# Picking fourteen embedding tables in teams of two, with shared compares, instead of fifteen one by one

## The reference, cut to what matters

```python
e = jnp.stack([tbl_0[ids[:, 0]], ..., tbl_31[ids[:, 31]]], axis=1)   # 512 x 32 x 128
dot = jnp.einsum('bnd,bmd->bnm', e, e)
flat = dot[:, iu, ju]                                               # pairs i < j
h = jnp.concatenate([flat, dense_ctx], axis=1)
h = jnp.maximum(h @ W_top1 + b_top1, 0.0)                            # 512 x 512
h = jnp.maximum(h @ W_top2 + b_top2, 0.0)                            # 512 x 256
y = h @ W_top3
```

## Time and profile before

| | |
|---|---|
| median of three runs without a profile | 124.33 us (123.89 to 124.69) |
| the profiled execution, first to last instruction | 148.7 us |
| busy in the profiled execution: PE, DVE, ACT, POOL | 121.4, 75.2, 78.8, 71.3 us |
| PE's mean granted clock, as a share of 2.4 GHz | 0.919 |

### The profile page before, as it was taken

The page is one execution under the profiler, slowest core; times in us unless marked ns, Lnnn a source line. Parts: engine busy times, 40 slices in busy tenths (PEclk is TensorE's granted clock), DMA queues, the critical chain, the costliest instruction groups (busy, mean ns, idle before and its releaser), DMA issues.

```text
span 148.7 us, 2677 instructions
## 1 busy us (share of the span) xinstructions
PE 121.4 (82%) x1028; PEld 99.5 (67%) x1028; DVE 75.2 (51%) x196; ACT 78.8 (53%) x79; POOL 71.3 (48%) x76
## 2 busy tenths in 40 slices
PE   5889979989999689499995464321999899999993
PEld 3457758868788468378884452111999798999971
DVE  2999999989897399496800000000333033223301
ACT  3588899999997897799950510000143302210022
POOL 3877749787787477378775577772000000000000
PEclk9999999999999999959999776555599999999999
DMA  5998736666667356793221011211056441024000
GB/s 144 275 338 267 234 100 204 204 216 225 217 219 235 110 178 195 232 324 113 55 53 52 23 53 53 53 53 35 4 146 202 136 126 35 4 78 127 10 0 1
DMA packets 11150, 19.81 MB, mean 133 GB/s; under 512 B 2353, under 2 KB 7473, under 8 KB 11138
## 3 DMA queue, kind: packets, MB, share of 16 engines
q1 hardware_dynamic: 7522, 13.74, 29.8%
q0 software_dynamic: 2176, 4.46, 10.3%
q10 hardware_dynamic: 1440, 1.44, 3.0%
HBM read 17.54 MB, written 2.13 MB: 132 GB/s over the span
## 4 chain that ended last, share of the span: by engine, by line
PE 64%; ACT 15%; issue 11%; another core or an unknown queue 5%; DVE 2%; DMA 2%; ACTq 0%
PE two_ps L564 15%; PE two_ps L566 14%; PE two_ps L606 8%; PE two_ps L625 8%; ACT onehot L442 8%; PE free_ps L606 7%; ACT emb L421 5%; PE free_ps L636 3%; PE turn_ps L574 3%; PE two_ps L636 2%; ACT high L421 2%; DMA id_sb<-row_ids 2%; PE two_ps L641 1%; PE turn_ps L625 1%
## 5 line engine op out<-in xcount | busy, mean ns | idle before, releaser
L307 POOL DMA_INDIRECT rows<-tables,row_no x64 | 66.6, 1040 | 26.5 <-issue 14.9
L564 PE MATMUL two_ps<-onehot,high 128*128 128x512 f32 x128 | 52.7, 412 | 7.4 <-ACT onehot L442 4.3
L566 PE MATMUL two_ps<-onehot,low 128*128 128x512 f32 x128 | 50.9, 397 | 0.0
L442 ACT ACTIVATE onehot<-narrow 128x2560 fp32r<-128x2560 f16 (+3 forms) x16 | 35.5, 2226 | 4.8 <-PE two_ps L566 3.0
L564 PEld LDWEIGHTS two_ps<-onehot,high 128*128 128x128 f32 x128 | 24.8, 193 | 16.7 <-issue 10.4
L566 PEld LDWEIGHTS two_ps<-onehot,low 128*128 128x128 f32 x128 | 24.8, 194 | 4.7
L326 DVE TENSOR_SCALAR onehot<-pick_id,own_row 128x512 fp32r<-128x512 int16 x53 | 23.0, 479 | 4.4 <-PE two_ps L566 3.5
L316 DVE TENSOR_TENSOR low<-home,high 128x512 fp32r<-128x512 f32 (+1 forms) x36 | 22.4, 625 | 3.8 <-issue 3.7
L336 DVE TENSOR_SCALAR narrow<-pick_id,own_row 128x512 f16<-128x512 int16 x75 | 22.4, 365 | 0.0
L606 PE MATMUL two_ps<-emb 128*64 128x64 f32 x240 | 12.9, 247 | 9.4 <-issue 9.3
L196 DVE COPY home<-free_ps 128x512 f32<-128x512 f32 x4 | 2.8, 692 | 33.8 <-remote 29.8
(11 more groups left out here) (37 smaller groups left out, 54.5 us busy)
## 6 DMA issues: line engine op xcount, KB each, us to landing
home<-picked SPq DMA_DIRECT2D x10, 512.0 KB, 3.6
home<-picked SPq DMA_DIRECT2D x4, 640.0 KB
pick_id<-pick_ids SPq DMA_DIRECT2D x13, 128.0 KB, 3.7
w_sb<-w SPq DMA_DIRECT2D x3, 512.0 KB
dot_out<-home SPq DMA_DIRECT2D x10, 128.0 KB, 2.4
rows<-tables,row_no POOLq DMA_INDIRECT x64
dot_out<-home ACTq DMA_DIRECT2D x6, 128.0 KB, 2.6
pairs<-dot_out SPq DMA_DIRECT2D x10, 64.0 KB, 2.0
```

The costliest lines, as they stand in the source:

```text
L307: pool.indirect_dma_start(rows[:, k % ROWS_HELD, i, :], None, lone if one_table else tables, bass.IndirectOffsetOnAxis(ap=id_sb[:, 0, c:c ...
L442: act.activation(onehot[:, at:at + n, :], narrow[:, t % 2, n0:n0 + n, :], ACT.Copy).then_inc(onehot_act, n)
L564: pe.matmul(out, high[:, at, D * k:D * (k + 1)], onehot[:, c % HOT, :], start=(k == 0), stop=False)
L566: pe.matmul(out, low[:, at, D * k:D * (k + 1)], onehot[:, c % HOT, :], start=False, stop=(k == KR[t] - 1)).then_inc(picked_done, 1)
```

## The change

Fourteen tables are picked (118 chunks, three of the tables with 10), and 18 are gathered. `MORE` becomes 2, so the first tile of a block has two gathers, a block has 18 and all have 72. Tile 13 now ends with gather 49, tile 14 with gather 53, the last one with 71.

The fourteen tables form eight teams: one table, six pairs, one table. A team's tables of equal chunk count go step by step together. One DVE compare of 1024 ids makes the one-hot matrices of both tables for a step, in either way; one id load serves a team. 68 steps are left. `BY_ACT` is 0 for the first team, 4 for one and 3 for the others: 22 steps. Two teams are held (`HELD`), three id sets, 8 one-hot steps and a ring of 7 narrow ones. `pace` counts steps. PE turns one tile in the middle and one at the end of a team. The last table's result is copied out in two parts, 128 samples by ACT and the rest by DVE. To save room, the narrow tile shares its place with `h1`, `h2` and the output row, and `w2` with the ids, so SP loads `w2` once DVE has made all its compares.

```diff
-PICK = 15
+PICK = 14
+TEAMS = [[0]] + [[t, t + 1] for t in range(1, PICK - 1, 2)] + [[PICK - 1]]
+KT = [KR[team[0]] for team in TEAMS]
...
-BY_ACT = [2, 4, 5, 5, 5, 5, 5, 5, 5, 5, 5, 6, 6, 6, 6]
+BY_ACT = [0, 3, 3, 3, 3, 3, 4, 3]
...
-TURNED = PICK - 1
-LAG = 2
-TABLES_HELD, IDS_HELD, HOT, ROWS_HELD = 3, 4, 16, 7
+TURNED = 2 * NT - 2
+HELD, IDS_HELD, HOT, NARROW, ROWS_HELD = 2, 3, 8, 7, 7
...
 def pace(c):
-    return min(51 * c // 20 - 10, CHUNK0[PICK])
+    blocks = min(51 * c // 20 - 10, CHUNK0[PICK])
+    return blocks if blocks < KT[0] else (blocks + KT[0]) // 2
...
+            for g in range(2, NT):
+                if g >= IDS_HELD:
+                    sp.wait_ge(onehot_dve, DVE0[g - IDS_HELD + 1])
...
+                ids_load(sp, g)
+                for i in range(len(TEAMS[g])):
+                    table_load(g, i)
...
+            sp.wait_ge(onehot_dve, DVE0[NT])
+            sp.wait_ge(narrow_ready, ACT0[NT])
             sp.dma_start(w2_sb[:, :, :], w2.rearrange("(c p) n -> p c n", p=P)).then_inc(weights_in, 16)
...
-                    dve.tensor_scalar(onehot[:, c % HOT, :], pick_id[:, t % IDS_HELD, :], own_row[:, i, k:k + 1], None,
+                    dve.tensor_scalar(onehot[:, c % HOT, 0:n, :], pick_ids_of[:, g % IDS_HELD, 0:n, :],
+                                      own_row[:, STEPS.index(KT[g]), k:k + 1], None,
                                       ALU.is_equal).then_inc(onehot_dve, 1)
...
-                    dve.tensor_scalar(narrow[:, t % 2, n, :], pick_id[:, t % IDS_HELD, :], own_row[:, i, k:k + 1], None,
+                    dve.tensor_scalar(narrow[:, at % NARROW, 0:n, :], pick_ids_of[:, g % IDS_HELD, 0:n, :],
+                                      own_row[:, STEPS.index(KT[g]), k:k + 1], None,
                                       ALU.is_equal).then_inc(narrow_ready, 1)
...
+            for g in range(1, NT):
+                if 1 < g < NT - 1:
+                    dve.wait_ge(pick_ids_in[g + 1], 16)
+                    make_narrow(g + 1)
+                if g >= HELD:
+                    dve.wait_ge(picked_done, STEP0[g - HELD + 1])
...
+            dve.wait_ge(pick_emb_ready, NT)
+            dve.tensor_copy(emb[:, BLK:B, F - 1], pick_ps[0][:, BLK:B]).then_inc(pick_emb_dve, 1)
...
+            for g in range(1, NT):
+                if g + 1 < NT:
+                    for i in range(len(TEAMS[g + 1])):
+                        split_high(g + 1, i)
+                if g >= 2:
+                    emb_out(2 * g - 4)
+                pick_out(g - 1)
+                if g + 1 < NT:
+                    make_onehots(g + 1)
+                if g >= 2:
+                    emb_out(2 * g - 3)
+            act.wait_ge(picked_done, STEP0[NT])
+            copy(emb[:, 0:BLK, F - 1], pick_ps[0][:, 0:BLK]).then_inc(pick_emb_ready, 1)
+            emb_out(2 * NT - 4)
...
+            def pick(g, k0, k1):
+                for k in range(k0, k1):
+                    step_waits(g, k)
+                    for i in range(len(TEAMS[g])):
+                        last = row_block(g, i, k)
+                    last.then_inc(picked_done, 1)
...
-            for t in range(PICK):
-                pick(t)
-                if t >= LAG:
-                    turn(t - LAG)
+            pick(0, 0, KT[0])
+            for g in range(1, NT):
+                if g >= 2:
+                    pe.wait_ge(pick_emb_ready, g - 1)
+                pick(g, 0, KT[g] // 2)
+                if g >= 2:
+                    turn(2 * g - 3)
+                pick(g, KT[g] // 2, KT[g])
+                turn(2 * g - 2)
             turn(TURNED - 1)
-            pe.wait_ge(pick_emb_ready, TWOS + 1)
+            pe.wait_ge(pick_emb_ready, NT)
             dot_group(0)
             turn(TURNED)
             dot_group(1)
+            pe.wait_ge(pick_emb_dve, 1)
             dot_group(2)
             dot_group(3)
```

More of the change, by code:

```diff
@@ L19 @@
 STEPS = sorted(set(KR))
+TEAMS = [[0]] + [[t, t + 1] for t in range(1, PICK - 1, 2)] + [[PICK - 1]]
+NT = len(TEAMS)
+KT = [KR[team[0]] for team in TEAMS]
+assert PICK % 2 == 0 and all(KR[t] == KT[g] for g, team in enumerate(TEAMS) for t in team)
+STEP0 = [sum(KT[:g]) for g in range(NT + 1)]
 PIECE = 2
 PIECES0 = KR[0] // PIECE
-LOW_CUT, HOT_CUT = [4, 4, 2], [3]
+LOW_CUT = [4, 4, 2]
 def cut(k, sizes):
@@ L77, with build @@
 PARTS = [(0, 2), (2, 3), (3, 4)]
[L80 removed]
+def build(nc, row_ids, pick_ids, tables, picked, context, w1, w2, small, lone, y):
     f32, f32r, i32, i16 = mybir.dt.float32, mybir.dt.float32r, mybir.dt.int32, mybir.dt.int16
@@ L363, in _ @@
[L363 to L387, removed]
@@ new lines, in _ @@
+            for g in range(1, NT):
+                if 1 < g < NT - 1:
+                    dve.wait_ge(pick_ids_in[g + 1], 16)
+                    make_narrow(g + 1)
+                if g >= HELD:
+                    dve.wait_ge(picked_done, STEP0[g - HELD + 1])
+                own = KT[g] - BY_ACT[g]
+                pieces = [(i, k0, k1) for k0, k1 in LOWS[g] for i in range(len(TEAMS[g]))]
+                n, made = len(pieces) - 1, 0
+                for j, (i, k0, k1) in enumerate(pieces):
+                    upto = max(own * j // n, 1 if g == 1 else 0)
+                    if g == 1 and j == 0:
+                        make_onehots(g, 0, 1)
+                        made = 1
+                    if k0 == 0:
+                        dve.wait_ge(high_ready, PIECES0 + TEAMS[g][i])
+                    split_low(g, i, k0, k1)
+                    make_onehots(g, DVE_K0[g] + made, DVE_K0[g] + upto)
+                    made = upto
+                    if g == 1 and j == 1:
+                        make_narrow(1)
+                if g == 1:
+                    dve.wait_ge(pick_ids_in[2], 16)
+                    make_narrow(2)
@@ L424, in relu, with split_high @@
                 return act.activation(out, sums, ACT.Relu, bias=bias[:, n:n + 1])
-            def split_high(t):
+            def split_high(g, i):
+                t = TEAMS[g][i]
                 act.wait_ge(table_in[t], 16)
[L428 to L442, removed]
-                    n0 += n
@@ L445, in pick_out @@
[L445 to L453, removed]
+                if g >= HELD:
+                    act.wait_ge(picked_done, STEP0[g - HELD + 1])
@@ new lines, in split_high, with make_onehots @@
+                copy(high[:, g % HELD, i, 0:width(t)], table[:, g % HELD, i, 0:width(t)]).then_inc(high_ready, 1)
+            def make_onehots(g):
+                act.wait_ge(narrow_ready, ACT0[g + 1])
+                n0, nt = 0, len(TEAMS[g])
+                while n0 < BY_ACT[g]:
+                    c, at = STEP0[g] + ACT_K0[g] + n0, ACT0[g] + n0
+                    n = min(BY_ACT[g] - n0, HOT - c % HOT, NARROW - at % NARROW)
+                    if c + n > HOT:
+                        act.wait_ge(picked_done, c + n - HOT)
+                    act.activation(onehot[:, c % HOT:c % HOT + n, 0:nt, :], narrow[:, at % NARROW:at % NARROW + n, 0:nt, :],
+                                   ACT.Copy).then_inc(onehot_act, n)
+                    n0 += n
```

173 lines of the change are left out of this document (77 added, 96 removed).

## The result

| | before | after |
|---|---|---|
| median without a profile | 124.17 us (123.89 to 124.69) | 129.32 us (127.72 to 129.67) |
| ratio, 95% interval | | 1.033 (1.026 to 1.039): slower |
| profiled execution: span, own time | 148.7, not known | 127.8, 129.67 us |
| granted PE clock, mean | 0.919 | 0.973 |

The change costs 3.3%. The forecast was 124.6 us, with 123.1 to 125.8 as its own range and 119.5 to 128.5 for all rivals together. The median lies 0.8 above even the wide range; taken by the ratio (1.033 x 124.33 = 128.4) the time lies just inside its upper end. Slower had a chance of 0.31. In the profiled execution 129.67 - 127.8 = 1.9 us lie outside the span; the prediction carried 2.7.

The account below looks back on a forecast made before the run. Bound by picking, then a chain on PE; after the change PE waits for tiles 13 and 14. Gather 53 landing at 77.8 + 0.44 for tile 14 + 43.7 chain + 2.7 constant = 124.6 us, range 123.1 to 125.8 (rivals 119.5 to 128.5).

Parts of the forecast that it names:

- the gather term: POOL's gathers: 31 starts at 47.2, 45 or 46 at 66, and 53 lands at 77.8, where tile 14 waits.
- the sum 77.8 + 0.44 + 43.7 + 2.7: Gather 53's landing, tile 14's transposes, PE's chain after it and the constant up to the median: 124.6 us.
- runs without a stop: POOL, no longer waiting for chunks during picking, issues gathers at 1.34 each up to 38, then at 1.26.
- Landing: Time from a gather's issue to its rows landing: 2.4 us, taken from a small store.
- The tail and the constant: PE's chain from the end of tile 14, 43.7 us as before, and 2.7 us carried along up to the median.
- Gathers have slack: In the kernel before, the last gather lands at 94.4 and PE wants it at 100.6.
- The 23 us of pauses: PE's pauses in the profiled execution, 23.2 us, taken as absent without a profile; picking then ends at 74.5.
- Gathers that keep up: Rival on POOL: gathers at 1.29 each, gather 53 lands at 74.2, time 121.0 us; chance 0.35.
- Long compares: Rival on POOL: gathers wait for whole, longer DVE compares, 1.465 each, gather 53 lands at 80.3: 127.1 us; chance 0.11.
- Half clock: Rival on PE: its second wait halves the clock over the next 3.4 us, losing 1.7: 126.3 us; chance 0.10.
- Lockstep: Rival in picking: ACT or DVE takes 5% more and teams wait; picking ends at 77, time 126.8; chance 0.07.
- no saving: Rival on DVE: shared compares cost double, DVE sets the pace, picking ends near 78: 127.8 us; chance 0.03.

Follow-up runs that it names:

- before, profiled again: The kernel before, without any edit, profiled once more: time 125.98 us, span 124.1.
- fourteen alone: The kernel before with fourteen tables picked one by one, 72 gathers, no teams, tile 12 turned at the end of picking: 125.5 us, ratio 1.001.
- teams, 68 gathers: The changed kernel without the second gather of each block's first tile (18th gathered table's rows left out): 126.7 us, ratio 1.015 to the kernel before.
- compares between: The changed kernel with a team's direct compares going 1, 1, 1, 2 between the low pieces in place of 0, 1, 2, 2: 127.07 us in one run.
- no pace: The changed kernel without POOL's waits for picked steps: 129.7 us, ratio 1.032 to the kernel before.
- POOL late: The changed kernel with POOL's first gather held until the first table piece is in: 129.69 us in one run.
- 68 gathers and moved tiles: The changed kernel with 68 gathers, tile 13 turned after group 0 and tile 14 after group 3: 121.5 us, ratio 0.976 to the kernel before.
- fifteen tables: The changed kernel with fifteen tables picked in teams, the last team a pair, and 68 gathers: 125.2 us, ratio 0.995 to the kernel before.
- split: The changed kernel with each compare of 1024 ids issued as two of 512: 138.3 and 147.3 us in two executions.
- both runs of fourteen alone: Fourteen tables one by one, 72 gathers, no teams: 125.5 us; the same with tiles 13 and 14 moved after groups 0 and 3: 122.4 us.

## Why the prediction was right or wrong

The mechanism of the forecast happened: picking gains 4 to 5 us, and PE gives them up waiting for tiles 13 and 14. It gives up more than it gained, so the size failed, above all that of the gather term. Laid beside the sum 77.8 + 0.44 + 43.7 + 2.7:

| term | predicted | measured | off by |
|---|---|---|---|
| gather 31 starts | 47.2 | 49.15 | +1.95 |
| between gathers 31 and 53 | 28.2 | 29.43 | +1.2 |
| issue of 53 to its rows | 2.4 | 3.48 | +1.1 |
| start of tile 14 to the end of the span | 44.1 | 45.7 | +1.6 |
| time outside the span | 2.7 | 1.9 | -0.8 |
| sum | 124.6 | 129.67 | +5.0 |

(75.4 - 47.2 = 28.2, and 127.8 - 82.06 = 45.7. The profiled run is the slowest of four; the median is 129.32.)

*Gather speed.* The step that failed is that POOL "runs without a stop" and so takes 1.414 and then 1.34 and 1.26 apiece. POOL ran almost without one (1.2 us beyond the gaps of 0.30, up to gather 31), but there was none to be saved: before, profiled again, has 0.2 us up to the same gather. The pace was the gathers' own duration beside a busy DVE, 1.145 and 1.137 between 20 and 50 us. Gather by gather, the streams of before and after lie together: gather 12 at 20.55 and 21.92, 20 at 33.77 and 32.82, 31 at 48.42 and 49.15, 45 at 68.30 and 68.56, 53 at 78.97 and 78.58. The change as a whole makes POOL's stream neither faster nor slower; the forecast had gather 53 at 75.4. With fourteen tables one by one it leaves at 74.70, and that kernel ends even, as forecast for the change. So the slower end belongs to teams and fourteen tables together: beside them a gather took 1.14, beside fourteen alone 1.00.

*Landing.* 2.4 came from a small store. A gather's median is 3.0 in after, and it varies: PE had the rows of tiles 12, 13 and 14 there 3.2, 2.7 and 3.5 us past the start of their last gather, and 2.5 to 4.4 over all runs in which it waited. At tile 14 it was 3.5 (after) and 3.7 (before, profiled again).

*The tail and the constant.* Both were derived from the disturbed profile. Before, profiled again, has 124.1 - 78.91 = 45.2 and 1.9, 47.1 together, where the sum had 46.8. After has 0.5 more in the tail. PE waits for ACT there, before group 4, where before again goes on without a gap, and gets part of it back at its next wait for ACT. ACT is late because its issue of two stores takes 2.25 us (the same pair took 1.28 in before again):

```profile
85.56 2.25 ACTq L210 DMA_DIRECT2D dot_out<-home  x2
89.08 2.08 PE L624 MATMUL free_ps<-emb 128*64 128x64 f32 x64 [0.62 <-ACT home L437]
```

What made that issue long stays open.

*"Gathers have slack."* This was worked out for the last tile alone, and from a profile in which PE stood still while POOL went on (busy 14 of 21 us). The kernel before has no slack at tile 14, where it waits 1.12, so the picking gain had nowhere to go. Read by difference from an undisturbed profile, the sum is short: tile 14 ends with gather 53 in place of 50, 78.58 against 75.23, +3.35, landing -0.2, tail +0.55, together 3.7; the spans differ by 127.8 - 124.1 = 3.7.

That the start of the gather that ends tile 14 sets the end holds within some 0.7 us across kernels with PE's order unchanged that wait for this tile:

| kernel | that gather starts | span | difference |
|---|---|---|---|
| before again | 75.23 | 124.1 | 48.9 |
| teams, 68 gathers | 73.23 | 122.7 | 49.5 |
| fourteen alone | 74.70 | 124.5 | 49.8 |
| compares between | 76.47 | 125.2 | 48.7 |
| after | 78.58 | 127.8 | 49.2 |
| no pace | 78.80 | 127.6 | 48.8 |
| POOL late | 79.47 | 127.9 | 48.4 |

It does not where PE asks for tile 14 later: with 68 gathers and moved tiles that gather starts at 74.61 and the span is 118.7, a difference of 44.1.

*What held.* The 23 us of pauses belonged to that one execution; picking ends at 74.4 (predicted 74.5) and 70 (70); the compares cost 0.77 and 0.48 (0.71 and 0.48); ACT is not late in the teams' middle. Shared compares made picking no shorter (74.96 against 74.4 with fifteen tables, 70.3 against 67.7 with fourteen). There was little to gain, as the sum of three windows from 20 to 74 us of before, profiled again, shows:

```profile
sum 54.00, PE 52.25 PEld 42.08 DVE 45.83 ACT 52.21 POOL 42.41; mean PE 17.42 PEld 14.03 DVE 15.28 ACT 17.40 POOL 14.14
```

PE was idle for 1.75 of 54 us: it set the pace of picking beside ACT, which the working had as the later one. And the ramp of the teams costs more than that: PE waits 1.84 and 1.31 for the first pair, and its matmuls are then 0.43 apart in place of 0.23 from 14.6 to 18.1, at the lower clock.

```profile
12.10 0.51 PE L577 MATMUL two_ps<-onehot,high 128*128 128x512 f32 x1 [1.84 <-DVE low L331]
14.62 0.67 PE L577 MATMUL two_ps<-onehot,high 128*128 128x512 f32 x1 [1.31 <-DVE onehot L340]
```

*The rivals.* Gathers that keep up: refuted for the change (1.475 apiece up to gather 31, not 1.29). Long compares: its 127.1 came nearer than the forecast, and it had the cadence nearly right (1.465), but its reason is not borne out: compares of 512 came with gathers of 1.145, 1.00 and, split, 2.48, compares of 1024 with 1.07 to 1.14. That it came near is luck. Half clock came after the first wait, of 3.84, and not the second (group 0 took 3.14 in place of 2.08), and was free: PE waited 1.64 for tile 14 anyway. Lockstep and no saving: not seen, PE has no gap from 20 to 70.

The Trainium skill, page "SBUF — State Buffer", section "Who interferes with whom", has the loser of the shared port blocked until the other engine's instruction ends. The split run has a gather of 8.75 us under DVE instructions of at most 0.7 us each: many instructions long, and not one. The estimate of 0.69 and 0.42 for the doubled compares, worked out in the prediction from the Trainium skill, page "VectorE: DVE Perf Modes", section "The TRN2 errata", was short of the 0.77 and 0.48 that were measured.

What stays open is what sets a gather's duration beside DVE, and with it why teams slow the gathers down with fourteen tables and not with fifteen. It isn't the pairing alone: between 20 and 50 us it is 1.145 before, 1.07 to 1.14 with teams in the order of after, and 1.00 in both runs of fourteen alone, whose DVE makes the same compares for a table as before. It isn't DVE's busy share, by the three windows above. In fourteen alone three gathers mostly take as long as DVE needs for a table, 3.84 us, so they fall at the same places of its sequence; that this makes them short is only argued. A shift of POOL's start by 1.9 us left the mean at 1.11.

## What to carry to other kernels

If a profile is 20% longer than the median, profile again before building on it: pauses of the one engine make the others look as if they had slack. Before counting a gain at the end of a phase, look for what the next step then waits for, and make the forecast as a difference of the same event (here, the gather that completes tile 14) in both kernels. Work that is moved to a slow stream must also be asked for later: fourteen tables one by one were even with the old order, and with two tiles turned later they gained 2.2%. And a change of two parts is best run in its parts: here neither part lost, the two together did.

## What the hardware showed unexpectedly

One gather of 128 rows took POOL from 0.94 us (DVE idle) to 8.75 us (beside DVE), and neither the length of DVE's instructions nor its busy share told which: beside compares of 512 the mean was 0.99 with DVE busy for 23.84 of 24 us (fourteen alone), and 1.91 with 24.00 (split compares). The rows were complete 2.5 to 4.4 us past the gather's start. And one profiled execution held 23 us of pauses on PE that the second profile of the same kernel, with its span of 124.1, doesn't have.
